# Cross-attention on one core: first half of a chunk's scores issued between projection and weighted sum, a third buffer of weights, the output projection beside the query projection

## The reference, cut to what matters

```python
x = layernorm(x)                       # (4, 256, 256), the queries' side
q = (x @ Wq)                           # 16 heads of 64
k = (context @ Wk); v = (context @ Wv) # context (4, 4096, 192)
sim = q @ k.T * 64 ** -0.5             # per head, 256 x 4096
out = softmax(sim) @ v                 # per head, 256 x 64
y = x + out.reshape(256, 1024) @ Wo + bo
```

## Time and profile before

| | |
|---|---|
| median of three runs | 2403.74 us (2401.39 to 2408.85) |
| the profiled execution | 2403.09 us, of which the span is 2401.3 us |
| mean granted clock of TensorE | 0.976 |
| TensorE matmul busy | 2123.0 us, 88% of the span |
| TensorE weight loads | 1549.2 us, 65% (beside matmuls) |
| VectorE | 1430.7 us, 60% |
| ScalarE | 1347.4 us, 56% |
| GpSimd | 1424.3 us, 59% |
| DMA | 79.95 MB, queue's share of 16 engines 11.2% |

### The profile page before, as it was taken

How to read it: one execution, slowest core, us unless ns; L and a number is a source line. 1 busy time by engine, 2 the same in 40 slices (tenths; PEclk the granted TensorE clock), 3 DMA queues, 4 the chain that set the end, 5 groups by cost and what they waited for, 6 DMA issues and landing times. The chain is left out here.

```text
span 2401.3 us, 51408 instructions
## 1 busy us (share of the span) xinstructions
PE 2123.0 (88%) x19830; PEld 1549.2 (65%) x19830; DVE 1430.7 (60%) x1630; ACT 1347.4 (56%) x1657; POOL 1424.3 (59%) x651
## 2 busy tenths in 40 slices
PE   4899999889999998899999988999999968665998
PEld 3577767666767676667676766776777744224777
DVE  5655555555555555555555555555555525997586
ACT  2466666666666666666666666666666662001341
POOL 0366666666666666666666656666666770553364
PEclk9899999999999999999999999999999989998999
DMA  7010001110101011101000111010000002000230
GB/s 218 13 28 18 25 13 38 43 28 15 27 17 29 13 38 43 31 20 26 13 25 13 38 43 32 19 26 13 25 13 17 4 8 111 0 0 9 88 115 35
DMA packets 44521, 79.95 MB, mean 33 GB/s; under 512 B 7040, under 2 KB 31104, under 8 KB 43536
## 3 DMA queue, kind: packets, MB, share of 16 engines
q1 hardware_dynamic: 44304, 76.67, 11.2%
HBM read 69.90 MB, written 5.31 MB: 31 GB/s over the span
## 5 line engine op out<-in xcount | busy, mean ns | idle before, releaser
L717 POOL TENSOR_TENSOR acc<-acc,PR 128x1024 f32<-128x1024 f32 x480 | 1150.0, 2396 | 536.0 <-ACT PR L523 514.1
L597 DVE TENSOR_REDUCE amx<-ps 128x2 f32<-128x1024 f32 x512 | 627.7, 1226 | 440.3 <-PE ps L307 440.3
L523 ACT ACTIVATE PR<-ps 128x1024 f32<-128x1024 f32 x512 | 500.9, 1023 | 228.9 <-PE ps L315 225.2
L482 ACT ACTIVATE ps<-NM 128x1024 f32<-128x1024 f32 x448 | 461.4, 1031 | 276.6 <-DVE V L582 232.7
L323 PE MATMUL ps<-PR,V 128*64 128x256 f32 x4096 | 501.9, 387 | 5.7 <-ACT PR L523 5.5
L323 PEld LDWEIGHTS ps<-PR,V 128*64 128x64 f32 x4096 | 271.9, 137 | 182.4 <-issue 46.6
L290 PE MATMUL ps<-wv,C 64*128 64x256 f32 x4608 | 330.2, 286 | 34.2 <-ACT PR L523 32.3
L290 PEld LDWEIGHTS ps<-wv,C 64*128 64x128 f32 x4608 | 307.2, 189 | 70.8 <-issue 43.8
L279 PE MATMUL ps<-C,wk 64*128 64x512 f32 x2304 | 321.8, 408 | 29.6 <-ACT PR L523 17.0
L315 PE MATMUL ps<-qh,KH 64*128 64x256 f32 x2048 | 313.3, 301 | 8.6 <-ACT ps L482 8.1
L315 PE MATMUL ps<-ql,KH 64*128 64x256 f32 x2048 | 293.0, 281 | 0.0
(11 more groups left out here) (164 smaller groups left out, 1747.4 us busy)
## 6 DMA issues: line engine op xcount, KB each, us to landing
wk<-wk_split SPq DMA_DIRECT2D x62, 192.0 KB, 3.2
wv<-wv_split SPq DMA_DIRECT2D x30, 384.0 KB, 5.1
bc<-wm_rows SPq DMA_DIRECT2D x16, 512.0 KB, 4.9
craw<-in_ctx SPq DMA_DIRECT2D x30, 256.0 KB, 3.8
we<-in_we SPq DMA_DIRECT2D x8, 768.0 KB, 7.6
wo<-in_wo SPq DMA_DIRECT2D x66, 64.0 KB, 2.2
wq<-in_wq SPq DMA_DIRECT2D x32, 128.0 KB, 2.4
craw<-in_ctx SPq DMA_DIRECT2D x30, 128.0 KB, 3.7
```

Of the source, the lines that this page charges most:

```text
L482: act.activation(ps[:, first_bank:first_bank + 2, :].rearrange("p h (k n) -> p h k n", k=2), row.unsqueeze(2).to_broadcast([P, 2, 2, ROWS] ...
L523: act.activation(PR[:, hf, :, :, :].rearrange("p h k n -> p (h k n)"), ps[:, banks[hf]:banks[hf] + 2, :].rearrange("p h n -> p (h n)"), AC ...
L597: dve.tensor_reduce(amx[:, :, t, c], psG, AX.X, ALU.max).then_inc(g_max, 1)
L717: pool.tensor_tensor(flat(acc[:, :, :, :]), flat(acc[:, :, :, :]), flat(PR[:, hf, :, :, :]), ALU.add).then_inc(acc_done, 1)
```

## The change

- The first half of the next chunk's scores moves from the head of step s+1 to step s, between projection and weighted sum (`scores_of(t + 1, 0)`), in all steps but the last of a pair. In step 0 the pair's own first half stays at the head.
- `PR` gets a third slot: first halves alternate between slots 0 and 1, second halves use slot 2. ScalarE's `weights` of the next first half moves behind the seed of the second half, ahead of a piece of context.
- `project_out` moves from the end of step 3 to step 0 of the next pair, behind `project_q` and ahead of the scores, into bank 6. Its weights' slots are swapped accordingly on SP's side, `add_rows` moves to step 0 on VectorE, and one more output projection (of a zeroed `Otn`) runs in the first pair.
- In step 0 the projection's low output goes into bank 5 and not into a score bank. It then waits for the split queries and the added rows and no longer for an exponential.
- Both parts of the queries are now made by VectorE (`split_q`), which takes line 473 off ScalarE. The reciprocal is written into `Otn`; `bo` lies in `acc`.
- `ROUNDS` is as before.

```diff
-        PR = sb("PR", [P, 2, 2, 2, ROWS])
+        PR = sb("PR", [P, 3, 2, 2, ROWS])
...
-        psN, psQ, psL, psX, psB, psO = ps[:, 4, :], ps[:, 5, 0:ROWS], ps[:, 4, 0:ROWS], ps[:, 5, :], ps[:, 6, :], ps[:, 7, 0:ROWS]
+        psN, psQ, psL, psX, psB, psO = ps[:, 4, :], ps[:, 5, 0:ROWS], ps[:, 4, 0:ROWS], ps[:, 6, :], ps[:, 6, :], ps[:, 7, 0:ROWS]
...
+        low_bank = lambda t: ps[:, 5 if t % NC == 0 else score_bank(t, 0), :]
+        pr_slot = lambda t, hf: 2 if hf else t % 2
...
-            load_wo(NC - 1, 1)
             load_wo(0, 0)
+            load_wo(1, 1)
...
-                load_wo(of_next(1), 1)
+                load_wo(of_next(0), 0)
...
-                    sp.wait_ge(out_ps, 2 * it + 2)
-                    load_wo(of_next(2), 0)
+                sp.wait_ge(out_ps, 2 * it + 2)
+                load_wo(of_next(1), 1)
...
@@ -386,14 +390,18 @@
                     def next_guess(n):
                         if n == 0:
                             pe.wait_ge(nm_sb, p + 1)
-                            pe.wait_ge(q_ready, p + 2)
+                            wait_drained(pe, it, t - 1, 0)
                         else:
                             pe.wait_ge(g_max, 16 * (p + 1) + n)
                         if n == 6:
                             pe.wait_ge(rl_ready, p + 1)
-                        if n == 8:
-                            pe.wait_ge(x_added, p + 2)
                         guess(p + 1, nslot, n)
+
+                    def scores_of(t, hf):
+                        c = CHUNK[t % NC]
+                        pe.wait_ge(k_lo, 2 * (4 * p + job_of(c)) + side_of(c) + 1)
+                        pe.wait_ge(seeded, 2 * (it * PER + t) + hf + 1)
+                        scores(pi, c, hf, score_bank(t, hf))
 
                     if s == 0:
                         pe.wait_ge(m_diag, p + 1)
@@ -403,12 +411,15 @@
                             if last and pi == 1:
                                 pe.wait_ge(xn_in, (b + 2) * 16)
                             project_q(nslot)
+                        pe.wait_ge(ot_ready, p + 1)
+                        pe.wait_ge(wo_in[pi], (it + 1) * 32)
+                        if has_job(t - 1, final):
+                            wait_drained(pe, it, t - 1, 1)
+                        project_out(pi)
+                        scores_of(t, 0)
                     if rounds[0] is not None:
                         next_guess(rounds[0])
-                    pe.wait_ge(k_lo, 2 * (4 * p + job_of(c)) + side_of(c) + 1)
-                    for hf in range(2):
-                        pe.wait_ge(seeded, 2 * T + hf + 1)
-                        scores(pi, c, hf, score_bank(t, hf))
+                    scores_of(t, 1)
                     if rounds[1] is not None:
...
-                        pe.wait_ge(p_ready, 2 * T + 1)
-                        wait_drained(pe, it, t - 1, 1)
-                        project(it, job, ps[:, score_bank(t, 0), :], psB,
+                        if s == 0:
+                            pe.wait_ge(q_ready, p + 2)
+                            pe.wait_ge(x_added, p + 2)
+                        else:
+                            pe.wait_ge(p_ready, 2 * T + 1)
+                            wait_drained(pe, it, t - 1, 1)
+                        project(it, job, low_bank(t), psB,
                                 (lambda: next_guess(rounds[2])) if rounds[2] is not None else (lambda: None))
                     elif rounds[2] is not None:
                         next_guess(rounds[2])
+                    if s < NC - 1:
+                        scores_of(t + 1, 0)
                     if pi == 0:
                         pe.wait_ge(v_sb, 2 * (8 * it + 2 * job_of(c) + 1) + side_of(c) + 1)
                     if s == 0:
                         pe.wait_ge(o_sb, p + 1)
                     for hf in range(2):
                         pe.wait_ge(p_ready, 2 * T + hf + 1)
-                        mm = weighted_sum(pi, c, hf, s == 0, s == NC - 1)
+                        mm = weighted_sum(pi, c, hf, pr_slot(t, hf), s == 0, s == NC - 1)
                     mm.then_inc(pv_done, 1)
...
                         row_sums()
-                    if s == 3:
-                        pe.wait_ge(ot_ready, p + 1)
-                        pe.wait_ge(wo_in[nslot], (it + 1) * 32)
-                        if more:
-                            pe.wait_ge(g_max, 16 * (p + 1) + 8)
-                        project_out(nslot)
...
-                    def weights(hf):
+                    def weights(t, hf):
+                        T, bank = it * PER + t, score_bank(t, hf)
                         act.wait_ge(s_ps, 2 * T + hf + 1)
-                        act.wait_ge(pv_done, T + 1)
+                        act.wait_ge(pv_done, T + hf + 1)
                         act.wait_ge(acc_done, 2 * T + hf + 1)
-                        act.activation(PR[:, hf, :, :, :].rearrange("p h k n -> p (h k n)"),
-                                       ps[:, banks[hf]:banks[hf] + 2, :].rearrange("p h n -> p (h n)"), ACT.Exp).then_inc(p_ready, 1)
+                        act.activation(PR[:, pr_slot(t, hf), :, :, :].rearrange("p h k n -> p (h k n)"),
+                                       ps[:, bank:bank + 2, :].rearrange("p h n -> p (h n)"), ACT.Exp).then_inc(p_ready, 1)
 
                     if t == 0:
                         act.activation(warm[:], zero[:], ACT.Exp)
@@ -532,13 +543,9 @@
                         if has_job(t - 1, final):
                             wait_drained(act, it, t - 1, 0)
                         seed(banks[1], row)
-                    weights(0)
-                    if s == 0:
+                        weights(t, 0)
                         act.activation(NM[:, :, :].rearrange("p h n -> p (h n)"), psN, ACT.Copy).then_inc(nm_sb, 1)
-                    weights(1)
-                    if s == 0 and more:
-                        act.wait_ge(q_ps, p + 2)
-                        scale_q(nslot)
+                    weights(t, 1)
...
-                        if job is not None:
+                        if job is not None and s > 0:
                             wait_drained(act, it, t, 0)
                         act.wait_ge(p_ready, 2 * T + 1)
                         seed(banks[0], NM[:, :, :])
+                        weights(t + 1, 0)
...
-            def split_q(slot):
+            def split_q(slot, pair):
+                dve.wait_ge(q_ps, pair + 1)
+                dve.tensor_scalar(qh[:, slot, :], psQ, float(DH) ** -0.5, None, ALU.mult).then_inc(q_hi, 1)
+                dve.wait_ge(q_hi, pair + 1)
                 dve.scalar_tensor_tensor(out=ql[:, slot, :], in0=psQ, scalar=float(DH) ** -0.5, in1=qh[:, slot, :].bitcast(F32),
...
-                dve.reciprocal(rl[:, :], psL).then_inc(rl_ready, 1)
+                dve.reciprocal(Otn[:, :], psL).then_inc(rl_ready, 1)
                 dve.wait_ge(rl_ready, pair + 1)
                 dve.wait_ge(o_sb, pair + 1)
-                dve.tensor_tensor(Otn[:, :], Ou[:, :], rl[:, :], ALU.mult).then_inc(ot_ready, 1)
+                dve.tensor_tensor(Otn[:, :], Ou[:, :], Otn[:, :], ALU.mult).then_inc(ot_ready, 1)
 
...
-                        dve.wait_ge(pv_done, T + 1)
+                        dve.wait_ge(pv_done, T + 2)
                         copy_o()
...
+            pool.memset(Otn[:, :], 0.0).then_inc(ot_ready, 1)
```

More of the change, by code:

```diff
@@ L66, in cross_attention @@
         xnT = sb("xnT_sb", [P, 2, ROWS])
-        bo = sb("bo_sb", [P, DM])
+        bo = acc[:, 0, 0, :]
         st6, mv, rs = sb("st6", [P, NR, 6]), sb("mv", [P, NR, 2]), sb("rs", [P, NR])
@@ L182, in _ @@
             load_ctx(0, 1, craw1, craw_in[1])
-            sp.dma_start(bo[:], d["bo"]).then_inc(c_in, 16)
+            sp.dma_start(bo, d["bo"]).then_inc(c_in, 16)
             for p in range(2):
@@ L317, in scores, with weighted_sum @@
                 mm.then_inc(s_ps, 1)
-            def weighted_sum(pi, c, hf, first, last):
+            def weighted_sum(pi, c, hf, slot, first, last):
                 for k in range(2):
@@ L322, in weighted_sum @@
                         hd = 2 * pi + h
-                        mm = pe.matmul(psO[half(h), :], V[:, c * KT + 2 * hf + k, hd * DH:hd * DH + DH], PR[:, hf, h, k, :],
+                        mm = pe.matmul(psO[half(h), :], V[:, c * KT + 2 * hf + k, hd * DH:hd * DH + DH], PR[:, slot, h, k, :],
                                        start=(first and hf == 0 and k == 0), stop=(last and hf == 1 and k == 1), skip_group_check=True)
@@ L345, in _ @@
                 mm = pe.matmul(psO[:, i * P:i * P + P], ones_r[:, :], ones_r[:, :], start=(i == 0), stop=(i == 1), skip_group_check=True)
-            mm.then_inc(pv_done, 1)
+            mm.then_inc(pv_done, 2)
             pe.wait_ge(xn_in, 16)
@@ L442, in quad @@
                         row_sums()
-                    if s == 3:
-                        pe.wait_ge(ot_ready, p + 1)
-                        pe.wait_ge(wo_in[nslot], (it + 1) * 32)
-                        if more:
```

(38 more changed lines are left out.)

6 lines of the change are left out of this document (removed).

## The result

The changed kernel takes **2470.1 us** (median of four, 2465.3 to 2477.2) against 2406.3 for the kernel before in the same comparison: ratio 1.027, 95% interval 1.0233 to 1.0307. It is slower, as forecast, but by 64 us and not by 17, and the range (up to 2442) doesn't hold it. The profiled execution has a span of 2472.7 us, 71.4 more than the one before; that is 7 more than the medians differ by, since of the changed kernel one of the longer executions was profiled (2474.5 us) and of the kernel before one of the shorter (2403.1).

The account below looks back on a forecast made before the run. TensorE's instruction order was taken to set the pace, so only its waits could change. Ordinary pairs +7.6, context pairs +9.2 and one more output projection +1.1 made 17.9 us: forecast 2421 us, range 2393 to 2442.

Parts of the forecast that it names:

- The waits of rows 2: TensorE's waits ahead of the two projections, 61.3 us in 29 pairs, nearly all released by the exponentials of line 523.
- In the last pair GpSimd's sums set the pace, and nothing changes: 0: Last pair: GpSimd's sums, 4.86 us for two, were taken to set the pace, so the change costs 0.
- the seed's margin for steps 4 to 6: ScalarE's seed for the early scores: ready after 3.2 us, needed by TensorE after 3.6, so covered by 0.4.
- These four waits are 0.95 longer each.: Three pairs taking in the next context: an exponential ahead of ScalarE's split lengthens four waits; +3.06 us a pair, +9.2 together.
- The ordinary pair, +0.27: Sum per ordinary pair of eight steps: -1.35 + 1.08 + 0.74 - 0.2 = +0.27 us; 28 such pairs give +7.6.
- A half of the scores, 0.75 us: Half the scores moves from each step's head to the end of the step before, 0.75 us, its work conserved.
- steps 1 and 2: With step 7: only half the scores stands between two rounds at least 1.83 us apart; +0.36 us in each.
- step 3: First round comes 2.65 us after the row sums, waiting for the reciprocal; with half the scores between, +0.74 us.
- Steps 4 to 6: The exponential freeing the projection's bank is issued a weighted sum earlier: -0.45 us in each, -1.35 together.
- "-0.2" for step 0: Step 0: the output projection fills waits but delays ScalarE's chain, with a 0.9 us seed wait; net -0.2 us a pair.
- number 5: Rival, chance 0.02: ScalarE's queue holds the early half behind the projection, the exponential's wait stays, nothing of 1.35 gained; 2463 us.
- Number 4: Rival, chance 0.07: seed or exponential margins missed by 0.3 in four steps behind a key projection; 37 us more, 2458.

## Why the prediction was wrong

**Right**: the sign, and the terms of the ordinary pair as mechanisms. The waits of rows 2 went; the distance between rounds (1.82) and between sums and round (2.65) stayed and turned into waits; the seed's wait in step 0 is 0.90 as worked out. The run with the rounds moved gave back 57 us, by a number set down beforehand. But these terms give little more than the sign: of the 70 us that the pairs account for, 54.7 are in the last two pairs and the three with context pieces, so a great part of the loss lies where I had put little or nothing.

**The step that failed outright: "In the last pair GpSimd's sums set the pace, and nothing changes: 0".** It was +20.8 us in the profiled execution, and +4.5 in pair 30; by medians, 16 us came back when the order there was restored. I had worked out the seed's margin for steps 4 to 6 myself, "TensorE needs it after 0.75 + 0.33 + 2.50", and 2.50 of that is a projection. The last ten steps have none, so the cover was gone; I looked at the engine that set the pace before and not at the new chain. I had not priced the clock either, and it makes half of the 20.8.

**"These four waits are 0.95 longer each."** In pair 14 three of them grew by 1.82 to 1.89 (3.15 to 5.03 the first), and the third by 2.16, counted with the wait of 0.84 ahead of the projection. The exponential was there, and a collision with GpSimd came on top, 0.96 each, which no term held: the piece shifted into GpSimd's sum. With the wait of 5 us the granted clock fell, 0.79 over 946 to 958 us, and the round behind it took 0.80 us instead of 0.50. +9.2 foreseen, +29.4 measured. This error is as large as that of the last pairs: the run with the piece ahead of the exponential gave back 30 us.

**The ordinary pair, +0.27, measured +0.57.** Of that, 0.44 is what pairs at full clock show. "A half of the scores, 0.75 us": two halves apart take 0.82 + 0.81 us where both together took 1.53. By the starts of pair 16, steps 1 and 2 grew by 0.5 and 0.4 instead of 0.36, and step 3 cost another 0.2, since the multiplication that GpSimd held up (1.08 us) stood ahead of the reductions. Steps 4 to 6 came out as foreseen, 1.31 us shorter against 1.35. 15.5 us instead of 7.6 in all.

**"-0.2" for step 0** was near in the changed kernel (-0.3), but it hid two terms of opposite sign. What changed in step 0 without the early half is worth 1.4 us a pair, and the early half takes back 1.1 of them, of which 0.9 is the wait for the seed. I never priced the parts apart. Of the change, all that is not the early half (measured with the piece ahead) gains 61 us, and the early half as placed, with its exponential ahead of the context piece, costs 125, both against the two kernels around it.

The rivals: number 5 was nearest in time (2463), by chance, for its mechanism did not occur: no wait is left ahead of the projections. Number 4, ScalarE late (2458), was wrong in place: the seeds were late, but in step 0 and where no projection stands, not behind key projections, and steps 4 to 6 were covered by the margins given.

## What to carry to other kernels

A margin is worked out over a cover, so list the steps in which that cover is missing (first, last, drained) and redo the margin there. Moving work out from between two instructions with a fixed distance turns full cover into a wait: look for start-to-start distances that equal a chain on another engine, even where no wait is shown. When instructions shift, ask for each of VectorE's with two SBUF inputs what GpSimd is doing at its new time.

## What the runs showed of the hardware

A VectorE multiplication of 128x256 elements with both inputs in SBUF, 0.42 us alone, took 2.54 us behind a GpSimd sum of 2.4 us that had started 0.13 before it, and a subtraction of 1.76 us took 2.72 at the median; without the sums it took 1.758. VectorE's 512 reductions out of PSUM took 1.21 to 1.23 us in both kernels, whatever GpSimd did. Across waits of 2.3 us a step in the last pair the granted clock was 0.76 on average in one execution and 0.90 in another, with up to 3.68 us for a weighted sum of 1.95; with waits of under 1 us in the same steps it was 0.96. In the three pairs with context pieces TensorE's idle time grew by 7.6 to 8.4 us and their length by 8.6 to 11.8; the most, 11.8, where the clock fell furthest (0.98 to 0.85). That the waits brought the clock down, and not something else, was not tested apart.
